# The last half sample's first transposing pass, moved from VectorE to TensorE

## The chip, the cores and the metric

The kernel runs on one core of one Trainium2 chip. The metric is device time in microseconds (us) for one execution of the whole program, the median of several runs; lower is better. A core has five engines with their own instruction queues (TensorE = PE, VectorE = DVE, ScalarE = ACT, GpSimd = POOL, SyncE = SP) and 16 DMA engines that all of them share. SP, ACT and POOL issue the transfers.

## What is computed

The reference runs four layers over 32 samples of 128 channels by 2048 positions, each with a residual:

```python
x = x + conv(x, L0_weight, groups=4, taps=9) + ctx0 + bias      # per-sample bias
x = x + (att1 @ weights1) x + bias1                             # a 1x1 convolution mixed from 8 kernels
x = x + (att2 @ weights2) x + bias2
x = x + conv(x, L3_weight, groups=4, taps=9) + ctx3 + bias
```

All is float32. The output is `out[32, 128, 2048]`, and what matters here is only how the last sample's last layer gets from PSUM to `out`.

## The kernel before

The samples are worked through one after the other, with TensorE always busy: the first grouped convolution (`conv0`), the two mixed layers as one product (`mix`), and the second convolution (`conv3`). TensorE writes the second convolution's result with partition = 32 output channels of a group by 4 phases of the position (position = 4 s + phase), group by group into PSUM banks. For most samples the result is turned into channel order by four DMA transfers (`relay_out`) and a GpSimd copy (`weave_out`) before it is stored.

For the last sample (number N - 1) there is nothing to hide this behind, so it goes another way, in two halves h of 1024 positions and four groups g of 32 channels each. `last_conv(h)` (L1052) ends the convolution; its result lies in `ps[:, last_bank(h) + g, 0:256]`. `turn_last(h)` on VectorE turns each piece by two passes of 32x32 block transposes: L885 (`ps` or `last_taps` into `last_mid`) and L888 (`last_mid` into `last_out`). Groups 2 and 3 are first evacuated with the bias by ScalarE (`evac_last`, L665); groups 0 and 1 are read from PSUM by VectorE, and get the bias after the second pass, in the first half from VectorE (`bias_first_half`, L895) and in the second half from ScalarE (`bias_last`, L672). In `last_out` partition 4 o + i holds positions 256 i to 256 i + 255 of the half for output channel o of the group. Each of the eight pieces (128 partitions of 1 KB, 128 KB) is stored by a transfer of its own: SP stores seven (`store_group`, L433), ScalarE's queue the last (L755).

Meanwhile ScalarE weaves the sample before the last in two copies (`weave_half`, L680) and GpSimd stores them (`store_woven`, L518), 512 KB each. Waits are semaphores written by hand, and each engine works in the order of its code. The program ends when SP has seen every store land (L446).

Of the kernel before, what the change touches and what calls it, by code (L numbers as in the profile page):

```python
# [57 lines left out]
def conditioned_residual_kernel(nc, x, cond, side, conv0_w, ctx0_w, mix1, mix2, conv3_w, ctx3_w, out):  # L58
# [9 lines left out]
    with ctx:  # L68
# [165 lines left out]
        last_evac = [sem(f"last_evac{h}") for h in range(2)]  # L234
        last_turned = [sem(f"last_turned{h}") for h in range(2)]
        last_runs = [sem(f"last_runs{h}") for h in range(2)]
        last_biased = [sem(f"last_biased{h}") for h in range(2)]
        woven_stored = sem("woven_stored")
        out_stored = [sem(f"out_stored{i}") for i in range(2)]

# [87 lines left out]
            return z_last if t.at(N - 1 - d) else (z_hi, z_lo)  # L328

        HALF = S // 2  # L330
        last_taps = x_in[0][:, 0:4 * HALF].rearrange("c (h g s) -> c h g s", h=2, g=2)
        last_mid = x_in[1][:, :].rearrange("c (h g s) -> c h g s", h=2, g=G)
# [25 lines left out]
        @block.sync  # L358
        def _(sp):
            def load_x(t, d):  # L360
                b = t.i + d
                if isinstance(b, int) and b - 2 < PLANED:
                    wait(sp, x_lo_done, b - 1)
                else:
                    sp.wait_ge(x_planed, b - 1 - PLANED)
                sp.dma_start(x_in[t.par(d)][:, :], x[b]).then_inc(x_loaded[t.par(d)], DMA)

            def relay_out(t, d, phases=range(PH)):
                b = t.i + d
# [48 lines left out]

            spread_mix_w(zero, 0, range(2))
            load_x(zero, 2)  # L420
            load_x(zero, 3)
            spread_mix_w(zero, 1)
            for t in ALL[1:N]:
                one(t)


            relay_out(ALL[N], -2, range(2))
            def store_group(h, g):
                if g >= 2:
                    sp.wait_ge(last_runs[h], g + 1)  # L430
                else:
                    sp.wait_ge(last_biased[h], g + 1)
                sp.dma_start(out[N - 1, rows(g), h * L // 2:(h + 1) * L // 2].rearrange("o (i x) -> o i x", i=RUNS),  # L433
                             last_out[:, h, g, :]).then_inc(out_stored[1], DMA)

            store_group(0, 2)
            store_group(0, 3)

            store_group(0, 0)
            store_group(0, 1)  # L440

            for g in range(G - 1):
                store_group(1, g)
# [88 lines left out]
        def _(act):  # L532
# [129 lines left out]
            def evac_last(h):  # L662
                for g in range(2, G):
                    act.wait_ge(last_conv_done[h], g + 1)
                    act.activation(last_taps[:, h, g - 2, :], ps[:, last_bank(h) + g, 0:HALF], ACT.Identity,  # L665
                                   bias=bias_tab[:, N - 1, G + g:G + g + 1]).then_inc(last_evac[h], 1)
# [79 lines left out]
            for t in ALL[1:N]:  # L746
                one(t)
            relay_last()
            evac_last(0)
            weave_half(0)  # L750
            weave_half(1)
            evac_last(1)
            bias_last()
            act.wait_ge(last_runs[1], G)
            act.dma_start(out[N - 1, rows(G - 1), L // 2:L].rearrange("o (i x) -> o i x", i=RUNS), last_out[:, 1, G - 1, :])\  # L755
               .then_inc(out_stored[1], DMA)

        @block.vector
        def _(dve):
# [114 lines left out]
                        low_x(t, 1)  # L874
                    low_z(t)

            def turn_last(h):
                for pair in (range(2), range(2, G)):
                    for g in pair:
                        if g >= 2:  # L880
                            dve.wait_ge(last_evac[h], g - 1)
                        else:
                            dve.wait_ge(last_conv_done[h], g + 1)
                        taps = last_taps[:, h, g - 2, :] if g >= 2 else ps[:, last_bank(h) + g, 0:HALF]
                        dve.transpose(blocks(last_mid[:, h, g, :]), taps).then_inc(last_turned[h], 1)  # L885
                    for g in pair:
                        dve.wait_ge(last_turned[h], g + 1)
                        dve.transpose(positions(last_out[:, h, g, :]), columns_of(last_mid[:, h, g, :]))\  # L888
                           .then_inc(last_runs[h], 1)

            def bias_first_half():
                for g in range(2):
                    dve.wait_ge(last_runs[0], g + 1)
                    o = last_out[:, 0, g, :]
                    dve.tensor_scalar(o, o, bias_tab[:, N - 1, G + g:G + g + 1], None, ALU.add)\  # L895
                       .then_inc(last_biased[0], 1)

            def second(t):
                low_y(t)
# [87 lines left out]
            second(ALL[1])  # L987
            for t in ALL[2:N]:
                one(t)
            turn_last(0)  # L990
            bias_first_half()
            turn_last(1)

        @block.tensor
        def _(pe):
# [44 lines left out]
            def last_conv(h):  # L1040
# [6 lines left out]
                for n in range(TURNS):  # L1047
# [3 lines left out]
                    for g in range(G):  # L1051
                        tile = pe.matmul(ps[:, last_bank(h) + g, 0:HALF], w[rows(g), d, :],  # L1052
                                         a[rows(g), d % PH, s:s + HALF], start=(n == 0), stop=(n == TURNS - 1))
                        if n == TURNS - 1:
                            tile.then_inc(last_conv_done[h], 1)

            def product(t, d):
                b = t.i + d
# [196 lines left out]
                one(t)  # L1255
            for h in range(2):
                last_conv(h)


_INS = ['x', 'cond_128', 'fside_S_0', 'L0_cond_weight', 'L0_cond_c_weight',  # L1260
# [25 lines left out]
```

## Time and profile before

| | us |
|---|---|
| median of 3 runs | 647.17 (646.9 to 647.23) |
| the profiled execution | 647.03 |
| its span in the profile | 645.2 |
| PE busy in the span | 634.8 (98%) |
| DVE busy | 500.8 (78%) |
| ACT busy | 357.1 (55%) |
| last matmul ends | 637.9 |
| last store is issued | 642.1 |

The table reads from the top: the profiled execution agrees with the median to 0.14 us, and 1.8 us of it lie outside the span. TensorE is busy until 637.9, and the last 7.3 us of the span hold the end that is changed.

### The profile page before, as it was taken

What the parts mean: (1) busy time and instruction counts of PE and PEld (TensorE: products, weight loads), DVE (VectorE), ACT (ScalarE), POOL (GpSimd) and SP (SyncE); (2) the same over time, 40 slices, a digit from 0 to 9 for tenths busy, and PEclk for the clock granted to TensorE, in tenths of its full rate; (3) what the DMA queues carried; (4) which work ended last, traced back from release to release, by engine and by line L of the source; (5) the groups of instructions that cost most, each with busy time, mean ns of one, the idle gap of its engine ahead of it and who ended that gap; (6) DMA issues with size and microseconds to landing.
All of it is one profiled execution on the core that took longest, in us unless ns stands there. A gap on an engine that the chain in (4) does not pass through costs nothing.

```text
span 645.2 us, 25168 instructions
## 1 busy us (share of the span) xinstructions
PE 634.8 (98%) x11218; PEld 624.0 (97%) x11218; DVE 500.8 (78%) x1002; ACT 357.1 (55%) x626; POOL 254.8 (39%) x99
## 2 busy tenths in 40 slices
PE   8999999999999999999999999999999999999995
PEld 6889999999999999999999999999999999999995
DVE  7897877787877787877787777787777787787736
ACT  4755546555546555546555645655645645645534
POOL 5024335534435534435534434534434533434220
PEclk9999999999999999999999999999999999999998
DMA  7345775555676554676555676555677545555515
GB/s 240 100 167 164 230 230 193 153 199 162 211 228 210 150 182 165 204 228 210 159 177 171 196 228 223 149 175 177 187 228 227 153 168 185 180 166 165 157 75 197
DMA packets 50329, 118.80 MB, mean 184 GB/s; under 512 B 5557, under 2 KB 26090, under 8 KB 42474
## 3 DMA queue, kind: packets, MB, share of 16 engines
q1 hardware_dynamic: 48882, 116.04, 56.5%
q10 hardware_dynamic: 920, 1.08, 0.6%
q0 software_dynamic: 480, 1.07, 0.4%
q8 instruction: 28, 0.46, 0.3%
q14 instruction: 19, 0.16, 0.1%
HBM read 35.33 MB, written 33.55 MB: 107 GB/s over the span
## 4 chain that ended last, share of the span: by engine, by line
PE 96%; DVE 2%; DMA 1%; ACT 1%; issue 0%; SPq 0%; POOL 0%; DVEq 0%; ACTq 0%; POOLq 0%
PE ps L1003 78%; PE ps L1093 14%; PE ps L1052 1%; PE ps L1078 1%; PE ps L1198 1%; DMA mix_w<-prod 1%; DVE x_in L885 0%; DVE acc L816 0%; DVE mat L816 0%; DVE x_planes L888 0%; ACT L714 0%; DVE x_hi L928 0%; PE ps L1132 0%; PE ps L1064 0%; SPq L387 0%
## 5 line engine op out<-in xcount | busy, mean ns | idle before, releaser
L467 POOL COPY out_sb<-out_planes 128x2048 f32<-128x2048 f32 x30 | 123.3, 4109 | 207.9 <-DVE mat2T_parts L825 187.0
L455 POOL COPY x_planes<-x_in 128x2048 f32<-128x2048 f32 x29 | 117.6, 4057 | 127.2 <-DVE x_lo L763 122.9
L787 DVE SCALAR_TENSOR_TENSOR z_lo<-ps,bias_tab,z_hi 128x1024 fp32r<-128x1024 f32 x62 | 76.8, 1280 | 62.1 <-ACT z_hi L585 62.1
L593 ACT ACTIVATE out_taps<-ps,bias_tab 128x512 f32<-128x512 f32 x62 | 39.3, 686 | 105.0 <-PE ps L1003 105.0
L1003 PE MATMUL ps<-z_hi,taps_lo 32*128 32x512 f32 x1488 | 97.4, 386 | 0.0
L777 DVE SCALAR_TENSOR_TENSOR y_lo<-ps,bias_tab,y_hi 128x512 fp32r<-128x512 f32 x128 | 87.2, 745 | 11.4 <-ACT y_hi L575 11.4
L1003 PE MATMUL ps<-x_lo,taps_hi 32*128 32x512 f32 x1536 | 94.8, 385 | 0.0
L1003 PE MATMUL ps<-x_hi,taps_lo 32*128 32x512 f32 x1536 | 94.8, 385 | 0.0
L1003 PE MATMUL ps<-x_hi,taps_hi 32*128 32x512 f32 x1536 | 94.4, 385 | 0.3 <-DVE x_hi L928 0.3
L1093 PE MATMUL ps<-y_hi,mix_w 32*128 32x512 f32 x1024 | 90.3, 385 | 0.8 <-DMA mix_w<-prod 0.8
L1003 PE MATMUL ps<-z_lo,taps_hi 32*128 32x512 f32 x1488 | 90.8, 385 | 0.0
L1003 PE MATMUL ps<-z_hi,taps_hi 32*128 32x512 f32 x1488 | 90.6, 384 | 0.0
L1003 PEld LDWEIGHTS ps<-x_hi,taps_hi 32*128 32x128 f32 x1536 | 86.3, 183 | 1.4 <-ACT taps_hi L599 0.6
L1003 PEld LDWEIGHTS ps<-x_lo,taps_hi 32*128 32x128 f32 x1536 | 86.4, 183 | 0.8
L1003 PEld LDWEIGHTS ps<-x_hi,taps_lo 32*128 32x128 f32 x1536 | 86.6, 183 | 0.6
L1003 PEld LDWEIGHTS ps<-z_lo,taps_hi 32*128 32x128 f32 x1488 | 84.0, 183 | 0.8
L1003 PEld LDWEIGHTS ps<-z_hi,taps_hi 32*128 32x128 f32 x1488 | 83.7, 183 | 0.7
L575 ACT ACTIVATE y_hi<-ps,bias_tab 128x512 fp32r<-128x512 f32 x128 | 77.1, 683 | 12.5 <-PE ps L1003 12.5
L1003 PEld LDWEIGHTS ps<-z_hi,taps_lo 32*128 32x128 f32 x1488 | 80.7, 183 | 0.9
L585 ACT ACTIVATE z_hi<-ps,bias_tab 128x1024 fp32r<-128x1024 f32 x62 | 65.9, 1114 | 25.8 <-PE ps L1093 25.8
L763 DVE TENSOR_TENSOR x_lo<-x_planes,x_hi 128x2048 fp32r<-128x2048 f32 x31 | 70.8, 2284 | 0.0
L833 DVE TENSOR_REDUCE prod_sum<-ps 128x128 f32<-128x1024 f32 (+2 forms) x31 | 35.4, 1143 | 42.9 <-PE ps L1078 37.5
(144 smaller groups left out, 711.3 us busy)
## 6 DMA issues: line engine op xcount, KB each, us to landing
x_in<-in_x SPq DMA_DIRECT2D x31, 1024.0 KB, 4.9
out_planes<-out_taps SPq DMA_DIRECT2D x122, 256.0 KB, 3.1
out<-out_sb SPq DMA_DIRECT2D x30, 1024.0 KB, 4.5
mix_w<-prod SPq DMA_DIRECT2D x126, 128.0 KB, 3.8
x_in<-in_x SPq DMA_DIRECT2D x2, 512.0 KB, 5.1
out<-out_sb POOLq DMA_DIRECT2D x2, 512.0 KB, 3.5
out<-x_planes SPq DMA_DIRECT2D x7, 128.0 KB, 3.0
out_taps<-in_L_cond_weight SPq DMA_DIRECT2D x1, 512.0 KB, 6.0
```

The source lines that it names most:

```text
L455: pool.tensor_copy(row_order(t, d, x_planes[:, :, :]), x_order(t, d, x_in[t.par(d)][:, :])).then_inc(x_planed, 1)
L467: pool.tensor_copy(x_order(t, d, out_sb[t.par(d)][:, :]), row_order(t, d, out_planes[:, :, :]))\
L575: act.activation(y_hi[:, g, :], ps[:, bank(t, 0) + g, :], ACT.Identity, bias=bias_tab[:, b, g:g + 1]).then_inc(y_hi_done, 1)
L585: act.activation(z_home(t, 0)[0][:, 2 * h:2 * h + 2, home(t, 0)], ps[:, k:k + 2, :], ACT.Identity, bias=bias_tab[:, b, 2 * G:BIAS]).then_i ...
L593: act.activation(out_taps[:, g, :], ps[:, bank(t, d) + g, :], ACT.Identity, bias=bias_tab[:, b, G + g:G + g + 1]).then_inc(out_act, 1)
L763: dve.tensor_tensor(out=x_lo[p][:, :, home(t, d)], in0=x_planes[:, :, :], in1=x_hi[p][:, :, home(t, d)].bitcast(F32), op=ALU.subtract).the ...
L777: dve.scalar_tensor_tensor(out=y_lo[:, g, :], in0=ps[:, bank(t, 0) + g, :], scalar=bias_tab[:, b, g:g + 1], in1=y_hi[:, g, :].bitcast(F32) ...
L787: dve.scalar_tensor_tensor(out=z_home(t, 0)[1][:, 2 * h:2 * h + 2, home(t, 0)], in0=ps[:, k:k + 2, :], scalar=bias_tab[:, b, 2 * G:BIAS], ...
L833: dve.tensor_reduce(out=prod_sum[:, :], in_=prod_at(t, d).rearrange("m r (h z) -> m z h r", z=C), axis=AX.XY, op=ALU.add).then_inc(prod_su ...
L1003: tile = pe.matmul(ps[:, first_bank + g, :], w[rows(g), d, :], a[rows(g), d % PH, c:c + S], start=(n == 0), stop=(n == TURNS - 1))
L1052: tile = pe.matmul(ps[:, last_bank(h) + g, 0:HALF], w[rows(g), d, :], a[rows(g), d % PH, s:s + HALF], start=(n == 0), stop=(n == TURNS - 1))
L1093: tile = pe.matmul(ps[:, bank(t, 0) + p, :], w[rows(p), g, h, :], a[rows(p), g, :], start=(n == 0), stop=(n == 3 * G - 1))
```

## The change

For the second half (h = 1) of the last sample:

- VectorE (groups 0 and 1) and ScalarE (groups 2 and 3) evacuate PSUM with the bias into `end_taps`, with the columns put in another order (`runs_apart`). VectorE's two evacuations are new, and ScalarE's two bias passes (L672) are gone.
- TensorE transposes each group in two 128x128 blocks with the identity (`pe.transpose`) into the banks of the first half. This takes the place of VectorE's four transposes of the first pass.
- VectorE makes the second pass alone, four block transposes that read PSUM.
- In `last_out` partition 32 i + o now holds run i of channel o. So the stores of this half name their destination as `i o x` (4 by 32 by 256), where it was `o i x` (32 by 4 by 256). Groups 0, 1 and 3 are stored by SP and group 2 by ScalarE's queue.

The first half is worked and stored as before.

```diff
+        def runs_of(taps):
+            return taps.rearrange("c (i j s) -> c i j s", i=RUNS, s=SQ)
+        def runs_apart(taps):
+            return taps.rearrange("c (j i s) -> c i j s", i=RUNS, s=SQ)
...
-            def store_group(h, g):
+            def store_first(g):
                 if g >= 2:
-                    sp.wait_ge(last_runs[h], g + 1)
+                    sp.wait_ge(last_runs[0], g + 1)
...
+            def store_end(g):
+                sp.wait_ge(last_runs[1], g + 1)
+                sp.dma_start(out[N - 1, rows(g), L // 2:L].rearrange("o (i x) -> i o x", i=RUNS),
+                             last_out[:, 1, g, :]).then_inc(out_stored[1], DMA)
...
-            def bias_last():
-                for g in range(2):
-                    act.wait_ge(last_runs[1], g + 1)
-                    o = last_out[:, 1, g, :]
-                    act.activation(o, o, ACT.Identity, bias=bias_tab[:, N - 1, G + g:G + g + 1])\
-                       .then_inc(last_biased[1], 1)
+            def evac_end():
+                for g in range(2, G):
+                    act.wait_ge(last_conv_done[1], g + 1)
+                    act.activation(runs_apart(end_taps[:, g, :]), runs_of(ps[:, last_bank(1) + g, 0:HALF]), ACT.Identity,
+                                   bias=bias_tab[:, N - 1, G + g:G + g + 1]).then_inc(end_evac[1], 1)
...
-            evac_last(1)
-            bias_last()
-            act.wait_ge(last_runs[1], G)
-            act.dma_start(out[N - 1, rows(G - 1), L // 2:L].rearrange("o (i x) -> o i x", i=RUNS), last_out[:, 1, G - 1, :])\
+            evac_end()
+            act.wait_ge(last_runs[1], G - 1)
+            act.dma_start(out[N - 1, rows(G - 2), L // 2:L].rearrange("o (i x) -> i o x", i=RUNS), last_out[:, 1, G - 2, :])\
...
+            def turn_end():
+                for g in range(2):
+                    dve.wait_ge(last_conv_done[1], g + 1)
+                    dve.tensor_scalar(runs_apart(end_taps[:, g, :]), runs_of(ps[:, last_bank(1) + g, 0:HALF]),
+                                      bias_tab[:, N - 1, G + g:G + g + 1], None, ALU.add).then_inc(end_evac[0], 1)
+                for g in range(G):
+                    dve.wait_ge(end_turned, g + 1)
+                    dve.transpose(positions(last_out[:, 1, g, :]),
+                                  ps[:, last_bank(0) + g, 0:HALF].rearrange("c (j o p) -> c j p o", o=SQ, p=PH))\
+                       .then_inc(last_runs[1], 1)
...
+            def turn_end():
+                for g in range(G):
+                    if g < 2:
+                        pe.wait_ge(end_evac[0], g + 1)
+                    else:
+                        pe.wait_ge(end_evac[1], g - 1)
+                    for j in range(2):
+                        at = slice(C * j, C * j + C)
+                        last = pe.transpose(ps[:, last_bank(0) + g, at], end_taps[:, g, at], ident[:, :])
+                    last.then_inc(end_turned, 1)
```

How the instructions stand on the engines at the end of the program: SyncE's queue before (`32x4x256` is the shape of the destination as the instruction carries it, slowest dimension first):

```order
L374 DMA out_planes<-out_taps 128x1x512
L433 DMA out<-x_planes 32x4x256 [waits last_runs0] x2
L433 DMA out<-x_planes 32x4x256 [waits last_biased0] x2
L433 DMA out<-x_planes 32x4x256 [waits last_biased1] x2
L433 DMA out<-x_planes 32x4x256 [waits last_runs1]
L68 UNCONDITIONAL_BRANCH [waits out_stored1,woven_stored,out_stored0]
```

and in the changed kernel:

```order
L384 DMA out_planes<-out_taps 128x1x512 x3
L389 DMA out<-out_sb 32x4x2048 [waits out_woven]
L384 DMA out_planes<-out_taps 128x1x512 [waits out_woven,out_dve,out_act]
L384 DMA out_planes<-out_taps 128x1x512
L443 DMA out<-x_planes 32x4x256 [waits last_runs0] x2
L443 DMA out<-x_planes 32x4x256 [waits last_biased] x2
L448 DMA out<-x_planes 4x32x256 [waits last_runs1] x3
L68 UNCONDITIONAL_BRANCH [waits out_stored1,woven_stored,out_stored0]
```

The number of stores is the same; the three of the second half no longer wait for a bias, and their destination's slowest dimension is 4 instead of 32.

VectorE's last instructions before (`x_planes` is `last_out`, `x_in` is `last_mid` or `last_taps`):

```order
L885 STREAM_TRANSPOSE x_in<-ps 128x8x8x4 [waits last_conv_done0] x2
L888 STREAM_TRANSPOSE x_planes<-x_in 128x2x4x32 [waits last_turned0] x2
L885 STREAM_TRANSPOSE x_in<-x_in 128x8x8x4 [waits last_evac0] x2
L888 STREAM_TRANSPOSE x_planes<-x_in 128x2x4x32 [waits last_turned0] x2
L895 TENSOR_SCALAR x_planes<-x_planes,bias_tab 128x256 [waits last_runs0] x2
L885 STREAM_TRANSPOSE x_in<-ps 128x8x8x4 [waits last_conv_done1] x2
L888 STREAM_TRANSPOSE x_planes<-x_in 128x2x4x32 [waits last_turned1] x2
L885 STREAM_TRANSPOSE x_in<-x_in 128x8x8x4 [waits last_evac1] x2
L888 STREAM_TRANSPOSE x_planes<-x_in 128x2x4x32 [waits last_turned1] x2
```

and in the changed kernel:

```order
L897 STREAM_TRANSPOSE x_in<-ps 128x8x8x4 [waits last_conv_done0] x2
L900 STREAM_TRANSPOSE x_planes<-x_in 128x2x4x32 [waits last_turned] x2
L897 STREAM_TRANSPOSE x_in<-x_in 128x8x8x4 [waits last_evac] x2
L900 STREAM_TRANSPOSE x_planes<-x_in 128x2x4x32 [waits last_turned] x2
L905 TENSOR_SCALAR x_planes<-x_planes,bias_tab 128x256 [waits last_runs0] x2
L910 TENSOR_SCALAR x_in<-ps,bias_tab 128x4x2x32 [waits last_conv_done1] x2
L914 STREAM_TRANSPOSE x_planes<-ps 128x2x4x32 [waits end_turned] x4
```

Behind the first half's work, eight transposes of the second half become two evacuations and four transposes.

ScalarE's last instructions before:

```order
L665 ACTIVATE x_in<-ps,bias_tab 128x256 [waits last_conv_done0] x2
L680 ACTIVATE out_sb<-out_planes 128x4x8x32 [waits out_stored0,out_relaid]
L680 ACTIVATE out_sb<-out_planes 128x4x8x32
L665 ACTIVATE x_in<-ps,bias_tab 128x256 [waits last_conv_done1] x2
L672 ACTIVATE x_planes<-x_planes,bias_tab 128x256 [waits last_runs1] x2
L755 DMA out<-x_planes 32x4x256 [waits last_runs1]
```

and in the changed kernel:

```order
L679 ACTIVATE x_in<-ps,bias_tab 128x256 [waits last_conv_done0] x2
L693 ACTIVATE out_sb<-out_planes 128x4x8x32 [waits out_stored0,out_relaid]
L693 ACTIVATE out_sb<-out_planes 128x4x8x32
L685 ACTIVATE x_in<-ps,bias_tab 128x4x2x32 [waits last_conv_done1] x2
L767 DMA out<-x_planes 4x32x256 [waits last_runs1]
```

The two evacuations keep their place behind the two weaving copies; the bias passes are gone.

## Rows read from the trace of the kernel before

**Rows 1.** The chain that ended last, from 636: start, us, what.

```profile
635.91 2.01 PE ps L1052 x60
637.93 1.14 DVE x_in L885 x2
639.06 0.92 DVE x_planes L888 x2
639.98 0.96 DVE x_in L885 x2
640.94 0.45 DVE x_planes L888
```

**Rows 2.** Timeline of the end: start, us, engine, line.

```profile
640.79 1.05 DVE L888 STREAM_TRANSPOSE x_planes<-x_in 128x256 f32<-128x256 f32 x2
...
639.18 0.85 ACT L665 ACTIVATE x_in<-ps,bias_tab 128x256 f32<-128x256 f32 x2
...
637.94 0.57 POOL L518 DMA_DIRECT2D out<-out_sb  x1 [19.43 <-ACT out_sb L680]
...
638.93 1.05 SPq L433 DMA_DIRECT2D out<-x_planes  x1
...
641.88 0.63 ACTq L755 DMA_DIRECT2D out<-x_planes  x1
```

**Rows 3.** Engines' busy time by stretch; last: PEclk, DMA share, GB/s.

```profile
638.00:640.00 2.00, 0.00 (x0) 0.00 (x0) 2.00 (x5) 2.00 (x4) 0.78 (x2) 1.00 0.76 279
640.00:640.50 0.50, 0.00 (x0) 0.00 (x0) 0.50 (x2) 0.50 (x3) 0.30 (x1) 0.74 1.00 393
...
638.80:644.40 5.60, 0.00 (x0) 0.00 (x0) 3.05 (x7) 2.02 (x5) 0.57 (x1) 0.63 0.96 351
...
644.50:645.20 0.70, 0.00 (x0) 0.00 (x0) 0.00 (x0) 0.00 (x0) 0.00 (x0) 0.50 0.00 0
```

**Rows 4.** DMA of 638.8 to 644.5: queue, packets, MB, share of 16 engines.

```profile
q0 software_dynamic: 288, 1.05, 46.4%
q1 hardware_dynamic: 864, 0.79, 41.4%
q10 hardware_dynamic: 144, 0.13, 6.6%
```

**Rows 5.** DMA of 638.0 to 638.8, one 128 KB store alone.

```profile
DMA packets 144, 0.13 MB, mean 164 GB/s; under 512 B 16, under 2 KB 144, under 8 KB 144
...
q1 hardware_dynamic: 144, 0.13, 49.3%
```

**Rows 6.** ScalarE's DMA queue in 0 to 8, and its transfers.

```profile
q10 hardware_dynamic: 200, 0.17, 8.0%
...
out_sb<-in_L_cond_weight ACTq DMA_DIRECT2D x1, 144.0 KB, 4.8
out_planes<-in_L_cond_b ACTq DMA_DIRECT2D x4, 0.5 KB
out_planes<-in_cond ACTq DMA_DIRECT2D x1, 16.0 KB, 4.9
```

**Rows 7.** DMA of 608.5 to 610.5, SBUF to SBUF: packets, MB, share.

```profile
q1 hardware_dynamic: 286, 0.31, 104.9%
```

**Rows 8.** Single lines: duration in ns (min/median/max), first and last start.

```profile
L895 DVE TENSOR_SCALAR x_planes<-x_planes,bias_tab x2: 309/328/347, 637.3 to 637.5; 128x256 f32<-128x256 f32 x2
...
L1132 PEld LDWEIGHTS ps<-ident,out_taps x8: 138/140/143, 15.3 to 16.0; 128*128 128x128 f32 x8
L1132 PE MATMUL ps<-ident,out_taps x8: 272/273/301, 15.3 to 16.1; 128*128 128x128 f32 x8
```

**Rows 9.** SP's stores of the last sample (L433).

```profile
L433 SPq DMA_DIRECT2D out<-x_planes x7: 539/602/1057, 637.0 to 642.1; - x7
...
DMA to landing us min/median/max: 2.1/3.0/3.3
```

More of the change, by code:

```diff
@@ L233, in conditioned_residual_kernel @@
         last_conv_done = [sem(f"last_conv_done{h}") for h in range(2)]
-        last_evac = [sem(f"last_evac{h}") for h in range(2)]
-        last_turned = [sem(f"last_turned{h}") for h in range(2)]
+        last_evac = sem("last_evac")
+        end_evac = [sem(f"end_evac{i}") for i in range(2)]
+        end_turned = sem("end_turned")
+        last_turned = sem("last_turned")
         last_runs = [sem(f"last_runs{h}") for h in range(2)]
-        last_biased = [sem(f"last_biased{h}") for h in range(2)]
+        last_biased = sem("last_biased")
         woven_stored = sem("woven_stored")
@@ L330, in conditioned_residual_kernel @@
         HALF = S // 2
-        last_taps = x_in[0][:, 0:4 * HALF].rearrange("c (h g s) -> c h g s", h=2, g=2)
-        last_mid = x_in[1][:, :].rearrange("c (h g s) -> c h g s", h=2, g=G)
+        last_taps = x_in[0][:, 0:2 * HALF].rearrange("c (g s) -> c g s", g=2)
+        end_taps = x_in[0][:, 2 * HALF:6 * HALF].rearrange("c (g s) -> c g s", g=G)
+        last_mid = x_in[1][:, 0:G * HALF].rearrange("c (g s) -> c g s", g=G)
         last_out = x_planes[:, :, :].rearrange("c p s -> c (p s)").rearrange("c (h g s) -> c h g s", h=2, g=G)
+        def runs_of(taps):
+            return taps.rearrange("c (i j s) -> c i j s", i=RUNS, s=SQ)
+        def runs_apart(taps):
+            return taps.rearrange("c (j i s) -> c i j s", i=RUNS, s=SQ)
         def blocks(mid):
@@ L427, in _ @@
             relay_out(ALL[N], -2, range(2))
-            def store_group(h, g):
+            def store_first(g):
                 if g >= 2:
-                    sp.wait_ge(last_runs[h], g + 1)
+                    sp.wait_ge(last_runs[0], g + 1)
                 else:
[L432 to L443, printed above, removed]
+                    sp.wait_ge(last_biased, g + 1)
+                sp.dma_start(out[N - 1, rows(g), 0:L // 2].rearrange("o (i x) -> o i x", i=RUNS),
+                             last_out[:, 0, g, :]).then_inc(out_stored[1], DMA)
+            def store_end(g):
+                sp.wait_ge(last_runs[1], g + 1)
+                sp.dma_start(out[N - 1, rows(g), L // 2:L].rearrange("o (i x) -> i o x", i=RUNS),
+                             last_out[:, 1, g, :]).then_inc(out_stored[1], DMA)
+            store_first(2)
+            store_first(3)
+            store_first(0)
+            store_first(1)
+            store_end(0)
+            store_end(1)
+            store_end(3)
             sp.wait_ge(out_stored[0], DMA * (N // 2 - 1))
@@ L660, in relay_last, with evac_last @@
                     act.dma_start(out_planes[:, p, :], out_taps[p:C:PH, :, :]).then_inc(out_relaid, DMA)
-            def evac_last(h):
+            def evac_last():
                 for g in range(2, G):
-                    act.wait_ge(last_conv_done[h], g + 1)
-                    act.activation(last_taps[:, h, g - 2, :], ps[:, last_bank(h) + g, 0:HALF], ACT.Identity,
-                                   bias=bias_tab[:, N - 1, G + g:G + g + 1]).then_inc(last_evac[h], 1)
-            def bias_last():
-                for g in range(2):
-                    act.wait_ge(last_runs[1], g + 1)
-                    o = last_out[:, 1, g, :]
-                    act.activation(o, o, ACT.Identity, bias=bias_tab[:, N - 1, G + g:G + g + 1])\
-                       .then_inc(last_biased[1], 1)
+                    act.wait_ge(last_conv_done[0], g + 1)
+                    act.activation(last_taps[:, g - 2, :], ps[:, last_bank(0) + g, 0:HALF], ACT.Identity,
+                                   bias=bias_tab[:, N - 1, G + g:G + g + 1]).then_inc(last_evac, 1)
+            def evac_end():
[3 more added lines that the diff above has]
+                                   bias=bias_tab[:, N - 1, G + g:G + g + 1]).then_inc(end_evac[1], 1)
             def weave_half(h):
@@ L748, in _ @@
             relay_last()
[L749 removed]
+            evac_last()
             weave_half(0)
             weave_half(1)
[L752 to L755 removed]
+            evac_end()
+            act.wait_ge(last_runs[1], G - 1)
+            act.dma_start(out[N - 1, rows(G - 2), L // 2:L].rearrange("o (i x) -> i o x", i=RUNS), last_out[:, 1, G - 2, :])\
                .then_inc(out_stored[1], DMA)
@@ L875, in one, with turn_first @@
                     low_z(t)
-            def turn_last(h):
+            def turn_first():
                 for pair in (range(2), range(2, G)):
@@ L880, in turn_last @@
                         if g >= 2:
-                            dve.wait_ge(last_evac[h], g - 1)
+                            dve.wait_ge(last_evac, g - 1)
                         else:
-                            dve.wait_ge(last_conv_done[h], g + 1)
-                        taps = last_taps[:, h, g - 2, :] if g >= 2 else ps[:, last_bank(h) + g, 0:HALF]
-                        dve.transpose(blocks(last_mid[:, h, g, :]), taps).then_inc(last_turned[h], 1)
+                            dve.wait_ge(last_conv_done[0], g + 1)
+                        taps = last_taps[:, g - 2, :] if g >= 2 else ps[:, last_bank(0) + g, 0:HALF]
+                        dve.transpose(blocks(last_mid[:, g, :]), taps).then_inc(last_turned, 1)
                     for g in pair:
[L887 to L891, printed above, removed]
+                        dve.wait_ge(last_turned, g + 1)
+                        dve.transpose(positions(last_out[:, 0, g, :]), columns_of(last_mid[:, g, :]))\
+                           .then_inc(last_runs[0], 1)
                 for g in range(2):
@@ L894, in bias_first_half @@
                     o = last_out[:, 0, g, :]
-                    dve.tensor_scalar(o, o, bias_tab[:, N - 1, G + g:G + g + 1], None, ALU.add)\
-                       .then_inc(last_biased[0], 1)
+                    dve.tensor_scalar(o, o, bias_tab[:, N - 1, G + g:G + g + 1], None, ALU.add).then_inc(last_biased, 1)
+            def turn_end():
[8 more added lines that the diff above has]
+                       .then_inc(last_runs[1], 1)
             def second(t):
@@ L989, in _ @@
                 one(t)
-            turn_last(0)
-            bias_first_half()
-            turn_last(1)
+            turn_first()
+            turn_end()
         @block.tensor
@@ L1257, in _ @@
                 last_conv(h)
+            turn_end()
 _INS = ['x', 'cond_128', 'fside_S_0', 'L0_cond_weight', 'L0_cond_c_weight',
```

## The prediction

> **What bounds the kernel now.** TensorE is busy 98% of the span, so only what lies behind its last matmul can change. I read the chain that ended last first: it follows TensorE to 637.9 and then VectorE's transposes one after the other [rows 1]. The last of them ends at 640.79 + 1.05 = 641.84, and ScalarE's queue issues the last store at 641.88 [rows 2]. By this view alone the end is VectorE's: eight transposes in 641.84 - 637.92 = 3.92 us, 0.49 each.
>
> The second view is the share of the DMA engines in the same stretch, and it says something else. From 638.8 to 644.4 all 16 are busy 96% of the time and move 351 GB/s [rows 3]. In these 5.6 us they carry two stores of 512 KB (the woven sample, issued by GpSimd) and seven of 128 KB [rows 4]. So the end has two limits that nearly meet: when the last piece is ready, and when the DMA engines have worked off their rows. The span ends about 0.75 us behind the last packet; no DMA engine is busy from 644.5 to 645.2 [rows 3].
>
> **What a store costs a DMA engine.** One store of 128 KB is 128 rows of 1 KB. The one that runs alone leaves 144 packets, 16 of them under 512 B [rows 5]: 128 rows, and one completion for each of 16 engines, so 8 rows each. Its packets took 49.3% of 16 x 0.8 us, that is 6.3 us, or 49 ns for a row. In the crowded stretch six such stores on SP's queue took 41.4% of 16 x 5.7 us = 37.8 us, 0.39 us for each engine and store, again 49 ns a row; the one on ScalarE's queue 6.6%, 6.0 us, 47 ns [rows 4]. A row costs a DMA engine the same alone and in a crowd. I take 48 ns.
>
> **The change, part by part.**
>
> *Evacuations on VectorE.* Two of 128x256 are added at its front. From SBUF such an operation took 0.33 us [rows 8]; from PSUM with the columns in another order I allow up to 0.45 each: done by about 638.6 to 638.8.
>
> *Evacuations on ScalarE.* They keep their place behind the weaving copies, and so their time: 639.18 to 640.03 [rows 2]. The other order of the columns may cost 0.1 us.
>
> *TensorE.* Two 128x128 transposes a group: a weight load of 0.14 us and 0.27 us for each [rows 8], of which neighbours overlap, so 0.4 to 0.6 us with the semaphores; groups 0 and 1 are hidden behind VectorE's own work. The granted clock is still 1.00 until 640 and averages 0.74 in the next half microsecond, 2.1 to 2.6 us behind the last matmul [rows 3], so the level of 1.2 GHz may meet groups 2 and 3, with matmuls of up to twice 0.27 us; that would be 0.3 us late, on a path that the DMA engines hide (below). Nothing is queued behind the new waits on TensorE.
>
> *VectorE's transposes.* Four instead of eight, at 0.49 us each. Groups 0 and 1 are ready at about 639.5 and 640.0, group 2 at 640.7. Group 3 waits for ScalarE (640.03) and TensorE (0.5), and ends at about 641.1 instead of 641.84. ScalarE's two bias passes go, which SP's stores of groups 0 and 1 waited for.
>
> *Stores.* The same eight on the same queues, the last issued 0.7 us earlier. SP is still busy issuing the first half's last store until 638.93 + 1.05 = 639.98 [rows 2], so it issues those of groups 0 and 1 at about 640.0 and 640.6. The bytes and the rows are the same, 128 of 1 KB, but the destination is written 4 by 32 by 256 where it was 32 by 4 by 256.
>
> **On how many DMA engines do these stores run?** This decides the sum. ScalarE's queue shows that the number follows the shape. In the first 8 us it issued the 144 KB load of 128 rows, the 16 KB one of 32 rows and four loads of one row, and left 200 packets [rows 6]. The first two are 128 + 16 and 32 + 16 packets if both use 16 engines, together 192. The other 8 are 2 for each one-row load: one row and a single completion. So a transfer of one row is cut to one engine, and those whose slowest dimension is 32 or 128 use all 16. No transfer from SP or ScalarE in the kernel before has a slowest dimension between 2 and 31, so 4 is not shown; its bounds are 4 engines and 16. I take 4, since the cut is seen to follow the count of the slowest dimension, and a program that deals 32 and 128 evenly to 16 has no even way to deal 4 to more than 4.
>
> The Trainium skill speaks to this: its page "DMA: Bandwidth & Descriptors", section "Why a DMA increments its semaphore by 16 and not by 1", says that the number of engines is the largest one up to 16 that divides the slowest dimension of both sides, as the instruction carries it, and that such transfers take the lowest-numbered engines. The one-row loads agree (one completion each). By that rule the four stores of the second half share the same four engines; without it the sum below would have no loss.
>
> **The sum.** Before, these four stores gave every engine 4 x 8 = 32 rows, 1.5 us. If they share four engines, each of those gets 4 x 32 = 128 rows, 6.1 us: 96 rows x 48 ns = 4.6 us more. The four engines are busy until then (96%), and the first of these stores is issued while the backlog stands (at 640.0 to 640.5 the share is 1.00 [rows 3]), so the extra work is added to their end almost one for one. What the earlier issue can give back is the idle 4% of 5.6 us, 0.2 us. Net +4.4 us: the last packet at about 648.9, the profiled execution at 647.03 + 4.4 = 651.4. The runs' median stands 0.14 us above the profiled execution, so I predict 651.5.
>
> Bounds of the price: 4 KB rows in the crowd cost 46.4% of 91.2 us for 1 MB, 41 ns a KB [rows 4]; if 1 KB rows come down to this once twelve engines are idle, 128 x 41 = 5.2 us replace 1.5, +3.5 net, 650.6. Upwards, a stretch filled mostly by transfers that write 1 KB rows into 32 SBUF partitions took 104.9% of 32 us for 0.31 MB, about 110 ns a KB [rows 7]: 14.1 us, +12.4 net. I take the price of the stores themselves, as they have the same bytes, direction and row length; only the step between an engine's rows differs (it was 4 KB runs, now 1 KB every 8 KB).
>
> **The rivals.**
>
> *A, 16 engines all the same.* For it: the bytes and the 128 source partitions are unchanged. Against: the one-row loads. Then VectorE's 0.7 us are won, but the DMA engines have 0.2 us of idle time to give: 646.8 to 647.0. Not slower.
>
> *B, VectorE's shorter work reaches the end in full.* Eight transposes (3.92) become two evacuations (0.66) and four transposes (1.96): -1.3 us, 645.9, at the edge of faster by 0.2%. It needs the 16-engine stores, ScalarE's evacuations not to be the last (they end at 640.03, against it), and DMA engines idle for 1.3 us of the last 5.6, where 0.2 is shown.
>
> *C, four engines and crowded rows.* If each engine's strided 1 KB rows meet the price of 110 ns: +12.4, 659.6. For it: it exists in this trace. Against: those rows are written into few SBUF partitions, and these go to memory.
>
> *D, TensorE and the extra hops are late.* At the low clock the last piece could be ready no sooner than now; with 16 engines this is 647.2, with four it changes nothing, since the backlog hides it. It falls in A or in my forecast.
>
> **How the numbers follow.** My forecast (four engines, 41 to 65 ns a row) has 0.84, A with D 0.10, C 0.04, B 0.02. Within 0.2% is about 1.3 us to either side, 645.9 to 648.5; a measurement of this kernel can tell no less from no change. So slower has 0.88, same 0.10, faster 0.02. The range follows the forecast: 649.6 (a little below 41 ns a row, and a gap less) to 653.6 (65 ns: 8.3 us in place of 1.5, less 0.2). It leaves out A, B, C and a few hundredths of the forecast, 2 in 10.
>
> **What the changed profile would show.** If right: the DMA share falls to about 4/16 = 0.25 from about 642.7 and stays there for about 6 us; the SP and ScalarE stores of the second half leave 32 rows per engine and 132 packets instead of 144; they land 4 to 8 us after issue, where 2.1 to 3.3 was usual [rows 9]; VectorE still ends near 641.1, and the wait at the end is SP's for the stores. If wrong: 144 packets and a share near 1 until 644.4 mean A; a share of 0.25 with far longer rows means C. A last VectorE transpose behind 641.9 would make my view of the TensorE part wrong, without moving the time.

## The result

| | us, median | ratio to before, 95% interval |
|---|---|---|
| before (6 runs of the same measurement) | 647.19 | |
| changed | 652.81 (652.3 to 653.26) | 1.0087, 1.0077 to 1.0097 |

The change makes the kernel 5.6 us slower, where 4.3 us were forecast (651.5, range 649.6 to 653.6). The time lies inside the range. The profiled execution took 652.79 us with a span of 651.0.

The chain of the changed kernel from 636 on (start, us, what) answers to [rows 1]:

```profile
635.99 2.24 PE ps L1071 x70
638.23 0.48 DVE x_in L910
...
638.76 0.45 PE ps L1086 x2
...
639.24 1.71 DVE x_planes L914 x3
```

The convolution ends at 638.23, 0.3 us later than in the execution before. From there the work the change was about is done sooner, as the timeline shows (start, us, engine; it answers to [rows 2]):

```profile
638.22 0.88 DVE L910 TENSOR_SCALAR x_in<-ps,bias_tab 128x256 f32<-128x256 f32 x2
...
638.76 0.83 PE L1086 MATMUL ps<-ident,x_in 128*128 128x128 f32 x4 [0.57 <-DVE x_in L910]
...
639.24 2.16 DVE L914 STREAM_TRANSPOSE x_planes<-ps 128x256 f32<-128x256 f32 x4
639.33 0.82 ACT L685 ACTIVATE x_in<-ps,bias_tab 128x256 f32<-128x256 f32 x2
...
639.84 0.80 PE L1086 MATMUL ps<-ident,x_in 128*128 128x128 f32 x4 [0.25 <-ACT x_in L685]
...
640.46 2.81 SPq L448 DMA_DIRECT2D out<-x_planes  x3
640.98 0.67 ACTq L767 DMA_DIRECT2D out<-x_planes  x1
```

VectorE ends at 639.24 + 2.16 = 641.40, 3.2 us behind the convolution instead of 3.9. Its four transposes follow each other almost without a gap. But the span goes on for 9.6 us more. The same stretch by windows (the last three columns are granted clock, DMA share of 16 engines, GB/s; it answers to [rows 3]):

```profile
641.00:642.00 1.00, 0.00 (x0) 0.00 (x0) 0.40 (x1) 0.00 (x0) 0.00 (x0) 1.00 0.92 331
642.00:643.00 1.00, 0.00 (x0) 0.00 (x0) 0.00 (x0) 0.00 (x0) 0.00 (x0) 0.71 1.06 391
643.00:644.00 1.00, 0.00 (x0) 0.00 (x0) 0.00 (x0) 0.00 (x0) 0.00 (x0) 0.50 0.49 61
644.00:645.00 1.00, 0.00 (x0) 0.00 (x0) 0.00 (x0) 0.00 (x0) 0.00 (x0) 0.50 0.20 56
645.00:646.00 1.00, 0.00 (x0) 0.00 (x0) 0.00 (x0) 0.00 (x0) 0.00 (x0) 0.50 0.27 89
646.00:647.00 1.00, 0.00 (x0) 0.00 (x0) 0.00 (x0) 0.00 (x0) 0.00 (x0) 0.50 0.27 85
...
648.00:649.00 1.00, 0.00 (x0) 0.00 (x0) 0.00 (x0) 0.00 (x0) 0.00 (x0) 0.50 0.28 97
...
650.00:651.00 1.00, 0.00 (x0) 0.00 (x0) 0.00 (x0) 0.00 (x0) 0.00 (x0) 0.50 0.01 4
```

No engine computes behind 641.4. Only the DMA engines are at work, and from 645 to 649 at a share of 0.27 to 0.28, a little over 4 of 16 (the times of an engine's packets overlap a little). ScalarE's queue, which issues one store of the second half, left 132 packets where its one store left 144 before [rows 4] (DMA of 636 to 651: queue, packets, MB, share):

```profile
q1 hardware_dynamic: 972, 0.92, 20.0%
q0 software_dynamic: 288, 1.05, 18.5%
q10 hardware_dynamic: 132, 0.13, 2.6%
```

132 is 128 rows and 4 completions. SP's seven stores left 972 = 4 x 144 + 3 x 132. So each of the four stores of the second half ran on four DMA engines, as forecast; and these are the same four for all, since the share stays at 0.28 or less while the stores of both queues are worked off. SP waits for them (its longest wait behind 636; in the kernel before the wait for the stores was 2.0 us):

```profile
SPq L460 <- DMA out<-x_planes: 7.2, 1, 7.2
```

### The profile page after: what moved, and what is told of

Same layout as the page of the kernel before. It is cut to its first block, busy times and chain, and to the rows that moved or that the text cites. A ratio compares the mean times of both kernels' runs of the same rounds, so it can differ in the third digit from the quotient of the medians.

```text
span 651.0 us, 25180 instructions
## 1 busy us (share of the span) xinstructions
PE 637.1 (98%) x11226; PEld 625.0 (96%) x11226; DVE 499.7 (77%) x1000; ACT 356.3 (55%) x624; POOL 253.1 (39%) x99
## 4 chain that ended last, share of the span: by engine, by line
PE 96%; DVE 2%; issue 0%; ACTq 0%; ACT 0%; POOL 0%; DVEq 0%; POOLq 0%
PE ps L1022 78%; PE ps L1125 13%; PE ps L1071 1%; PE ps L1230 1%; PE ps L1110 1%; DVE y_lo L789 0%; ACTq L621 0%; DVE x_planes L914 0%; DVE acc L828 0%; DVE mat L828 0%; PE ps L1164 0%; PE ps L1203 0%; PE ps L1096 0%; ACT y_hi L589 0%; DVE x_lo L780 0%
## 5 line engine op out<-in xcount | busy, mean ns | idle before, releaser
L589 ACT ACTIVATE y_hi<-ps,bias_tab 128x512 fp32r<-128x512 f32 x128 | 77.0, 682 | 12.9 <-PE ps L1022 10.9
```

The source lines that it names most:

```text
L589: act.activation(y_hi[:, g, :], ps[:, bank(t, 0) + g, :], ACT.Identity, bias=bias_tab[:, b, g:g + 1]).then_inc(y_hi_done, 1)
```

## The experiments

Two things were to be told apart: whether the whole loss is the stores' and not the new hops over TensorE, and whether it is the number of DMA engines or something else about where the rows lie. Then: where the forecast's missing 1.2 us went, and what became of VectorE's gain. Each ratio is to the kernel before, run in the same measurement. The second half's convolution ended at different moments in the profiled executions, from 637.6 (the new work alone) to 638.4 (far rows); a difference of less than a microsecond between two profiles has to be read from there.

### Stores alone

The kernel before with the new form of the destination (and the same for ScalarE's store):

```diff
-                sp.dma_start(out[N - 1, rows(g), h * L // 2:(h + 1) * L // 2].rearrange("o (i x) -> o i x", i=RUNS),
-                             last_out[:, h, g, :]).then_inc(out_stored[1], DMA)
+                place = out[N - 1, rows(g), h * L // 2:(h + 1) * L // 2]
+                place = place.rearrange("o (i x) -> o i x", i=RUNS) if h == 0 else place.rearrange("o (i x) -> i o x", i=RUNS)
+                sp.dma_start(place, last_out[:, h, g, :]).then_inc(out_stored[1], DMA)
```

> The kernel before, with nothing changed but the destination of the four stores of the second half, written 4 by 32 by 256 where it was 32 by 4 by 256. The rows land at other places, so the second half of the last sample comes out in another order. Engines theory (my forecast: such a store runs on 4 DMA engines, 48 ns a row, and nothing else matters): the four stores leave 132 packets each, the DMA share falls to about 0.25 behind 642.7, and the time is 4.5 to 6.0 us above before, about 0.5 above the changed kernel or equal to it. Compute theory (the loss of 5.6 us comes from the new hops over TensorE and PSUM): the time is that of before, 647.2, within 0.5.

Measured: 653.44 us, ratio 1.0099 (1.0084 to 1.0115), before 647.17. ScalarE's queue left 132 packets. This is the whole loss and 0.6 us more, without any of the new work: +6.3 us, where I expected 4.5 to 6.0.

### The new work alone

The changed kernel with the old form of the destination (and the same for ScalarE's store):

```diff
-                sp.dma_start(out[N - 1, rows(g), L // 2:L].rearrange("o (i x) -> i o x", i=RUNS),
+                sp.dma_start(out[N - 1, rows(g), L // 2:L].rearrange("o (i x) -> o i x", i=RUNS),
```

> The changed kernel with all its new work on VectorE, ScalarE and TensorE, and the four stores of the second half written 32 by 4 by 256 as before, so the second half of the last sample comes out in another order. Engines theory: 144 packets a store, the DMA share stays near 1 until 644, the last VectorE transpose ends near 641.4 and the time is 0.1 to 0.6 us below before (647.2), 646.6 to 647.1. Compute theory: the time stays at that of the changed kernel, 652.8, within 0.5.

Measured: 647.24 us, ratio 1.0001 (0.9992 to 1.001). Windows of its profile:

```profile
643.00:644.00 1.00, 0.00 (x0) 0.00 (x0) 0.00 (x0) 0.00 (x0) 0.00 (x0) 0.50 0.99 340
644.00:645.00 1.00, 0.00 (x0) 0.00 (x0) 0.00 (x0) 0.00 (x0) 0.00 (x0) 0.50 0.23 78
```

All 16 DMA engines stay nearly full until 644, as before. The compute theory has fallen: the new work costs nothing that the time shows. It gains nothing either (I expected 646.6 to 647.1): what VectorE wins, the stores lose. SP's three stores of the second half took 3.4 to 3.7 us from issue to landing, where 2.1 to 3.3 was seen before [rows 9]:

```profile
DMA to landing us min/median/max: 3.4/3.6/3.7
```

### Far rows on 16 engines

The kernel before, the four stores each as 128 rows of 1 KB, 8 KB apart (shown for ScalarE's; SP's three take the same `end_place`):

```diff
+        def end_place(g):
+            return out[N - 1, :, L // 2 + 256 * g:L // 2 + 256 * g + 256]
...
-            act.dma_start(out[N - 1, rows(G - 1), L // 2:L].rearrange("o (i x) -> o i x", i=RUNS), last_out[:, 1, G - 1, :])\
+            act.dma_start(end_place(G - 1), last_out[:, 1, G - 1, :])\
```

> The kernel before with its four stores of the second half written as 128 rows of 1 KB, each 8 KB behind the other (every one of the 128 channels, 256 positions), so the rows land at other places and the second half comes out in another order. Engines theory: slowest dimension 128, 16 engines, and the time is that of before, 647.2, within 0.5. Rival (the distance between an engine's rows in memory is what costs, not the number of engines): the time is up to 5.6 us above before, with rows well over 48 ns at a DMA share near 1.

Measured: 648.18 us, ratio 1.0017 (1.0008 to 1.0026). The distance of the rows is not the 5.6 us. But the time is 1.0 us above before, twice what I allowed. The profile shows a part of it only: that execution took 1.3 us more than the profiled one of before (648.34 against 647.03), but its convolution had already ended 0.5 us later (638.4 against 637.9), which leaves 0.8 us for the end. So the distance may cost most of the microsecond, and how much is not shown. Against the stores alone (653.44), whose rows lie just as far apart, 16 engines in place of four are 5.3 us faster: this is the number of engines at the same distance.

### Eight engines and two

The kernel before again, with destinations whose slowest dimension is 8 (the first half's stores then go to channels 64 to 127, with 16 channels by 8 runs):

```diff
+        def end_place(g):
+            return out[N - 1, 16 * g:16 * g + 16, :].rearrange("o (i x) -> i o x", i=8)
```

or 2:

```diff
+        def end_place(g):
+            return out[N - 1, 64 * (g // 2):64 * (g // 2) + 64, L // 2 + 512 * (g % 2):L // 2 + 512 * (g % 2) + 512].rearrange("o (i x) -> i o x", i=2)
```

> The kernel before with the destinations of the four stores of the second half written 8 by 16 by 256 (and those of the first half as 16 whole channels of 8 runs each, which is near and even on 16 engines); the last sample comes out in another order. Engines theory: each of the four stores leaves 128 + 8 packets, on 8 engines; the engines used get 64 rows in place of 32, 32 x 48 ns = 1.5 us more, and up to 1 us for the far rows seen with 16 engines: 648.5 to 649.8. If the number of engines fell to 4 for anything but 16: 651.5 to 653.5. If it stayed at 16 and only the distance of the rows counted: 648.2.

> The kernel before with the destinations of the four stores of the second half written 2 by 64 by 256; the second half comes out in another order. Engines theory: 2 engines, 130 packets a store, 256 rows each in place of 32, 224 x 48 ns = 10.8 us more, with the DMA share at 0.125 for about 12 us: 657 to 660. If a price per row that falls as fewer engines are at work: 655 or less.

Measured: eight 648.76 us, ratio 1.0018 (1.0000 to 1.0035); two 657.59 us, ratio 1.0164 (1.0150 to 1.0178); before 647.25. ScalarE's queue in the profile of the kernel with eight:

```profile
q10 hardware_dynamic: 136, 0.13, 2.0%
```

and in that with two:

```profile
q10 hardware_dynamic: 130, 0.13, 1.9%
```

and two of its windows:

```profile
643.00:645.00 2.00, 0.00 (x0) 0.00 (x0) 0.00 (x0) 0.00 (x0) 0.00 (x0) 0.50 0.15 24
...
647.00:649.00 2.00, 0.00 (x0) 0.00 (x0) 0.00 (x0) 0.00 (x0) 0.00 (x0) 0.50 0.14 48
```

128 rows and 8, and 128 rows and 2 completions. With two, 48 GB/s go over two engines for ten microseconds behind 645: 24 GB/s each, the same as the 97 GB/s over four of the changed kernel, and hardly more than the 341 GB/s over 16 (21 each) of the kernel before in 643 to 644. Twelve or fourteen idle engines make the others little faster. The rows of the busiest engine and the time stand like this:

| slowest dimension | engines | rows of the busiest engine | more than before | 48 ns a row | measured |
|---|---|---|---|---|---|
| 32 (before) | 16 | 32 | 0 | 0 | 0 |
| 8 | 8 | 64 | 32 | 1.5 us | +1.5 us |
| 4 (stores alone) | 4 | 128 | 96 | 4.6 us | +6.3 us |
| 2 | 2 | 256 | 224 | 10.8 us | +10.4 us |

Eight and two agree with the forecast's price to 0.4 us. Four is 1.7 us above it. But the interval of eight reaches from nothing to 2.3 us, and the agreement of two is luck: two errors cancel. At 24 GB/s a row costs an engine 43 ns, not 48, so 256 rows take 10.9 us in place of the 1.5 of before, +9.4. And from 643 to 645 the two engines moved only 24 GB/s in all, half of what they moved later, which loses 1.0 us: together +10.4. The same slow stretch is there with the stores alone (28 GB/s in 643 to 644) and, weaker, with eight engines (149 GB/s in 643 to 644, then 193).

### Without the woven sample's stores

The three kernels without the two 512 KB stores (that sample is then missing from the output):

```diff
-            sp.wait_ge(woven_stored, 2 * DMA)
...
-            store_woven(0)
-            store_woven(1)
```

> The kernel before without the two 512 KB stores of the woven sample (the one before the last), which is then missing from the output; ScalarE still weaves it. The DMA engines are relieved of half of the bytes of the end. If before is bound by the DMA engines at the end: about 1 us below before, 646.2. If it is bound by VectorE's chain and the last store's own 2.5 us: within 0.4 us of before, 646.8 to 647.2.

> The compute-only kernel (work of the change, stores written 32 by 4 by 256) without the two 512 KB stores of the woven sample. If the 0.7 us by which the last piece is ready sooner were lost only because the DMA engines are full: 0.5 to 0.8 us below the kernel before without those stores. If the gain was not there at all: equal to it within 0.3 us.

> The changed kernel without the two 512 KB stores of the woven sample, which is then missing from the output. Behind 643 the changed kernel had rows of 1 KB that moved at 61 and 56 GB/s before they settled at 97 GB/s, about 1 us lost that the forecast's sum didn't have. If this stall comes from the woven rows and the piled-up stores meeting: without them the four engines start at about 641.4 with nothing before them and need 128 x 46 ns = 5.9 us, last packet at 647.3, time 649.7 to 650.2, with no stretch under 90 GB/s once all four stores are queued. If the stall belongs to four engines alone: 650.7 or more, with the same slow stretch. If the slow stores did not depend on the number of engines at all: 645.6, as the compute-only kernel without the woven stores.

Measured, in us:

| | with the woven stores | without |
|---|---|---|
| before | 647.17 | 646.36, ratio 0.9985 (0.9976 to 0.9994) |
| the new work, old form of the stores | 647.24 | 645.59, ratio 0.9975 (0.9965 to 0.9985) |
| changed | 652.81 | 650.02, ratio 1.0042 (1.0028 to 1.0055) |

Before came to lie 0.8 to 0.9 us lower, near the 1 us that I gave for an end bound by the DMA engines; the other two are within what was expected for them.

Two things follow. The new work is 0.8 us faster than the old once the DMA engines have room; with them full it is worth nothing. That these 0.8 us are VectorE's gain, which was 0.7 us in the changed kernel, is not shown: in the two profiled executions without the woven stores (646.36 and 645.99, only 0.4 apart) VectorE ended at 641.78 and 641.63, and in the second it had waited 0.4 us for TensorE behind ScalarE, whose weaving ended later. The stores land in 2.1 to 2.3 us in both; in the profile of the new work:

```profile
out<-x_planes SPq DMA_DIRECT2D x7, 128.0 KB, 2.1
out<-x_planes ACTq DMA_DIRECT2D x1, 128.0 KB, 2.2
```

And the form of the stores costs 650.02 - 645.59 = 4.4 us here, against 652.81 - 647.24 = 5.6 us with the woven stores. So the forecast's missing microsecond comes up only beside the woven stores. This is no pure price of slow rows, since without these stores the end of the 16-engine kernel isn't set by full DMA engines (share 0.51 in 642 to 643). The profile of the changed kernel without them:

```profile
642.00:643.00 1.00, 0.00 (x0) 0.00 (x0) 0.00 (x0) 0.00 (x0) 0.00 (x0) 0.50 0.27 77
643.00:644.00 1.00, 0.00 (x0) 0.00 (x0) 0.00 (x0) 0.00 (x0) 0.00 (x0) 0.50 0.27 94
644.00:645.00 1.00, 0.00 (x0) 0.00 (x0) 0.00 (x0) 0.00 (x0) 0.00 (x0) 0.50 0.27 83
645.00:646.00 1.00, 0.00 (x0) 0.00 (x0) 0.00 (x0) 0.00 (x0) 0.00 (x0) 0.50 0.27 78
646.00:647.00 1.00, 0.00 (x0) 0.00 (x0) 0.00 (x0) 0.00 (x0) 0.00 (x0) 0.50 0.27 95
```

The stretch at 61 and 56 GB/s is gone, but there are still slices of 77 to 83 GB/s, so my "no stretch under 90" was wrong. What is missing to 97 GB/s adds up to 0.6 us here (642 to 647), and to 1.0 us in the changed kernel (643 to 647), so by the windows the woven stores explain about half of the slow rows.

### The whole output on 16 engines

The new layout keeps a run in 32 partitions, so a store can take one run with its 32 channels as the slowest dimension. Three kernels have the changed kernel's work, with other stores. By run and pair of groups, eight of 64 KB:

```diff
+        def store_runs(eng, pair, runs):
+            eng.wait_ge(last_runs[1], 2 * pair + 2)
+            for i in runs:
+                at = L // 2 + i * L // 8
+                eng.dma_start(out[N - 1, 2 * GC * pair:2 * GC * pair + 2 * GC, at:at + L // 8]
+                              .rearrange("(g o) x -> o g x", g=2),
+                              last_out[rows(i), 1, 2 * pair:2 * pair + 2, :]).then_inc(out_stored[1], DMA)
```

> The changed kernel with its four stores replaced by eight of 64 KB: one for each run i and pair of groups, from the 32 partitions of that run, written 32 by 2 by 256, two runs on SP and two on ScalarE's queue for each pair. The whole output is computed. Engines theory: the slowest dimension is 32 on both sides, so each runs on 16 engines (64 rows and 16 completions, 80 packets); rows per engine are again 32 in all, and the time is that of the compute-only kernel up to 0.5 us above it for the four more issues of 0.6 us each, 646.7 to 647.4, so no slower than before. A rival, that the permuted layout itself costs the DMA engines (a run's source is one quarter of the partitions, so the engines read the same 32 partitions and its rows take 110 ns as in the stretch at 608.5): each engine's 32 rows cost 3.5 us in place of 1.5, and the time is about 649.

Eight stores of 64 KB to near rows (the second half's order is another):

```diff
+                g, a = 2 * pair + i // 2, i % 2
+                at = GC * g + 16 * a
+                eng.dma_start(out[N - 1, at:at + 16, L // 2:L].rearrange("o (i x) -> o i x", i=RUNS),
+                              last_out[64 * a:64 * a + 64, 1, g, :]).then_inc(out_stored[1], DMA)
```

> The changed kernel's work with eight stores of 64 KB as in the by-run kernel, on the same queues and at the same waits, but each from 64 partitions of one group to 16 neighbouring channels, so every DMA engine writes 4 KB in one stretch of memory, as before; the second half comes out in another order. If the by-run kernel's 1.2 us above before come from where its rows lie in memory (8 KB apart): 647.0 to 647.5. If they come from issuing eight stores instead of four: 648.3 as there.

And four of 128 KB, one for each run with all groups, behind the last transpose:

```diff
+        def store_runs(eng, runs):
+            eng.wait_ge(last_runs[1], G)
+            for i in runs:
+                at = L // 2 + i * L // 8
+                eng.dma_start(out[N - 1, :, at:at + L // 8].rearrange("(g o) x -> o g x", g=G),
+                              last_out[rows(i), 1, :, :]).then_inc(out_stored[1], DMA)
```

> The changed kernel with its four stores cut another way: one for each run i with all four groups, from the 32 partitions of that run, written 32 by 4 by 256, two on SP and two on ScalarE's queue, all behind the last transpose. The whole output is computed. Slowest dimension 32 on both sides, so 16 engines, 144 packets each. They come when the woven stores are just worked off: last pieces issued at 641.3 and 641.9, 4 x 8 rows x 48 ns = 1.5 us on every engine, last packet near 644.3. If the number of stores is what cost the by-run and the halves kernels their 1 us: 647.0 to 647.5, that is, all of the change's loss is mended, with no gain. If far rows cost it: 648.0 to 648.4.

| | us | ratio to before |
|---|---|---|
| by run and pair, eight stores | 648.35 | 1.0024 (1.0014 to 1.0034) |
| halves, eight stores, near rows | 648.25 | 1.0015 (1.0006 to 1.0024) |
| by run, four stores | 647.86 | 1.0008 (0.9999 to 1.0017) |

The four stores by run compute the whole output and take back 5 of the 5.6 us; their interval includes no difference from before, and their time lies between what I gave for the one cause (647.0 to 647.5) and for the other (648.0 to 648.4), so they don't decide between them. None of the three beats before. The eight near stores are as slow as the eight far ones, so the idea that far rows make the by-run kernel's 1.2 us is wrong for the larger part. For the by-run kernel itself both of my expectations missed: 646.7 to 647.4 by the engines theory, 1.0 us too low, and 649 by the rival with 110 ns a row, 0.7 us too high. In the profile of the four stores by run (before, 643 to 644 had a share near 1 as well, but at 341 GB/s):

```profile
642.00:643.00 1.00, 0.00 (x0) 0.00 (x0) 0.00 (x0) 0.00 (x0) 0.00 (x0) 0.50 1.04 370
643.00:644.00 1.00, 0.00 (x0) 0.00 (x0) 0.00 (x0) 0.00 (x0) 0.00 (x0) 0.50 0.94 245
644.00:645.00 1.00, 0.00 (x0) 0.00 (x0) 0.00 (x0) 0.00 (x0) 0.00 (x0) 0.50 0.88 284
```

Here too the rows slow down behind 643, with 16 engines at work; in the by-run kernel with eight stores it is 240 GB/s at a share of 0.94.

## Why the prediction was right, and where its size was off

*What bounds the end.* Right, and it is what decided. The chain showed VectorE; the share of 0.96 showed that the DMA engines had no room. (The last store to be issued in the kernel before was SP's, at 642.1 [rows 9], not ScalarE's at 641.88; the sum doesn't use it.) The new work alone is worth 0.0 us beside the woven stores and 0.8 us without them.

*The evacuations, TensorE and the transposes.* VectorE's evacuations took 0.48 us each and 0.88 for both (up to 0.45 each was allowed), ScalarE's kept their time, and VectorE ended 3.2 us behind the convolution, as summed. The wait for ScalarE and TensorE came before group 2's transpose instead of group 3's, and cost only about 0.1 us. The clock did not fall before TensorE's transposes: it was 1.00 until 642, and they took 0.27 to 0.33 us each.

*The number of engines.* Right: 132, 136 and 130 packets with 4, 8 and 2 as the slowest dimension. The rule cited from the Trainium skill's page "DMA: Bandwidth & Descriptors" (section "Why a DMA increments its semaphore by 16 and not by 1") agrees in all of these. That the four stores share their engines is shown by the share of 0.27.

*The price of a row.* The term "96 rows x 48 ns = 4.6 us" is the one that was mis-sized: 6.3 us by the stores alone, 5.6 us by the two kernels with the new work, 4.4 us by the same pair without the woven stores. It has two errors of opposite sign. At the steady 24 GB/s an engine, a row costs 43 ns, so 128 rows take 5.5 us, 0.6 less than the sum had. What the sum had not at all is a slow stretch: what is missing to 97 GB/s is worth 1.0 us in the changed kernel (643 to 647) and 1.2 us with the stores alone (643 to 648). Together this gives 5.0 to 5.2 us; the rest of the 5.6 and 6.3 has no place in the windows. Most of the stretch lies between 643 and 645 of the changed kernel's profile (DMA of that stretch; the first line is its GB/s in 40 slices of 0.05 us):

```profile
GB/s 164 246 164 123 62 102 21 0 0 21 62 61 0 0 0 20 41 41 41 41 21 61 21 21 21 21 61 82 41 41 61 41 82 61 61 61 61 61 123 123
...
q1 hardware_dynamic: 114, 0.10, 28.7%
```

and in 647 to 650:

```profile
q1 hardware_dynamic: 236, 0.23, 22.1%
```

114 packets on SP's queue took 28.7% of 32 us, 9.2 us, 81 ns each; later 236 took 22.1% of 48 us, 45 ns each. The 81 ns are a mean: in the slices of 0.05 us there are up to three in a row in which no row began on any of the four engines, so single rows were held up for long (the longest record of a row there has 0.7 us, where 46 ns is usual). That the woven rows have a part in it is made likely by leaving them out. Why rows are held up just there is open. It comes with two, four and eight engines, with eight stores instead of four, and to a lesser degree with four stores by run; it doesn't come in the kernel before and with the new work alone. All kernels that show it write the second half's rows by another cut or to other places than these two.

*What the earlier issue gives back.* I had 0.2 us, the idle share. The stores alone at the old issue times took 653.44, the changed kernel 652.81: 0.6 us. The two profiled executions took the same time (652.76 and 652.79), but in the second the convolution ended 0.4 us later, which gives 0.4 us. An explanation that no run tests: four engines start their backlog when the first pieces come, and that is earlier by what VectorE wins. The error has the other sign than the one above, and hid a part of it. The two medians come from different measurements and their ranges overlap, so 0.4 to 0.6 us is no more than a likely size.

*The rivals.* A (16 engines) is what the new work alone shows, with the form put back: 647.24 in place of 646.8 to 647.0. B is what it does when the DMA engines have room: 0.8 us, not 1.3. C (110 ns a row throughout) is out: 24 GB/s an engine is 43 ns a KB. D is out too: VectorE ended at 641.40, before the 641.9 that I named as its sign. Of the signs I named, the time from issue to landing of the four stores stays unread, as the profile gives none for stores on fewer than 16 engines. SP began to issue its last one at 641.7, and rows still moved behind 650, so it landed more than 8 us later, beyond the 4 to 8 that I gave.

## What to carry to other kernels

Write the slowest dimension of a store's destination so that all 16 DMA engines get a share, as 32 or 128 did here, even when the layout in SBUF suggests another order: the same bytes in the same number of transfers cost 6.3 us more with a 4 in front. Count the completion packets of a queue in the profile; they tell how many DMA engines a form uses. And where work ends in stores, look at the share of the DMA engines before crediting a shorter chain: at 0.96 a chain shorter by 0.5 to 0.7 us was worth nothing.

## What the runs showed of the hardware that was not expected

- A DMA engine moves 1 KB rows at nearly the same speed whether 2, 4 or all 16 are at work: 24, 24 and 21 GB/s (48 over two, 97 over four, 341 over 16). So the time of these stores follows the rows of the busiest engine, 43 to 48 ns each, as long as no row is held up.
- Far rows cost about 1 us with 16 engines (ratio 1.0017), eight stores instead of four about as much (1.0015). Neither was seen in a price per row before the runs, and the cause of both is open; a part of the first may lie ahead of the stores, as the profile has it.
- The granted clock fell at very different times behind the last matmul. In the kernel before it averaged 0.74 in 640.0 to 640.5 [rows 3], 2.1 to 2.6 us behind it. In the far-rows kernel, which has the same work on TensorE and ended it at 638.4, it stood at full speed until 643, 4.6 us behind, as its windows show. So the later fall in the changed kernel (1.00 until 642) can't be put down to its eight transposes.

```profile
642.00:643.00 1.00, 0.00 (x0) 0.00 (x0) 0.36 (x1) 0.00 (x0) 0.00 (x0) 1.00 1.06 415
643.00:644.00 1.00, 0.00 (x0) 0.00 (x0) 0.00 (x0) 0.00 (x0) 0.00 (x0) 0.50 0.97 346
```
